# A four-layer graph network on one core: VectorE's one-hot order in the first layer's edge loop

## The reference, cut to what matters

```python
xl = (x @ W_l + b_l).reshape(n, HEADS, C);  xr = (x @ W_r + b_r).reshape(n, HEADS, C)
e = (edge_attr @ W_e).reshape(-1, HEADS, C)
g = jax.nn.leaky_relu(xl[src] + xr[dst] + e, 0.2)
logits = jnp.einsum('ehc,hc->eh', g, att)
ex = jnp.exp(logits - segment_max(logits, dst)[dst])
alpha = ex / (segment_sum(ex, dst)[dst] + 1e-16)
out = segment_sum(xl[src] * alpha[..., None], dst) + bias
```

## Time and profile before

| | |
|---|---|
| runs of the kernel | 6460.43, 6465.83, 6470.49 us (median 6465.83) |
| the profiled execution | 6478.12 us, its span 6476.2 us |
| the edge loop, first gather to last | 438.3 to 2844.3 us, 28 turns of 85.9 us |
| busy over the whole span | PE 78%, weight loads 67%, DVE 46%, ACT 28%, POOL 60% |
| TensorE's mean granted clock | 0.731 of full, over the whole span |

### The profile page before, as it was taken

The page is one execution under the profiler, slowest core; times in us unless marked ns, Lnnn a source line. Parts: engine busy times, 40 slices in busy tenths (PEclk is TensorE's granted clock), DMA queues, the critical chain, the costliest instruction groups (busy, mean ns, idle before and its releaser), DMA issues. The chain is left out here.

```text
span 6476.2 us, 113947 instructions
## 1 busy us (share of the span) xinstructions
PE 5047.6 (78%) x35178; PEld 4313.9 (67%) x35178; DVE 2978.9 (46%) x3937; ACT 1845.2 (28%) x3914; POOL 3856.6 (60%) x3427
## 2 busy tenths in 40 slices
PE   2328888888888888870799967888787788885899
PEld 2315665666555665550799967778777777774899
DVE  7657877777777777755422131111111111112321
ACT  0015555555555455530000002222222222221100
POOL 5747887888888888853000017777777777776000
PEclk9667888888888888865899975555555555555799
DMA  9325555555555555531799946666667666664598
GB/s 358 83 79 141 154 144 148 155 153 144 149 150 152 142 152 153 155 97 36 259 366 366 364 143 215 202 206 201 201 204 208 207 205 204 205 209 122 228 397 329
DMA packets 622991, 1260.53 MB, mean 195 GB/s; under 512 B 131705, under 2 KB 431290, under 8 KB 597220
## 3 DMA queue, kind: packets, MB, share of 16 engines
q10 hardware_dynamic: 217740, 649.85, 31.5%
q1 hardware_dynamic: 295768, 492.49, 21.2%
q0 software_dynamic: 109184, 115.05, 8.6%
HBM read 923.85 MB, written 490.51 MB: 218 GB/s over the span
## 5 line engine op out<-in xcount | busy, mean ns | idle before, releaser
L697 POOL DMA_INDIRECT att_gl<-tab_l,top_zero x1568 | 1928.4, 1230 | 488.5 <-issue 475.6
L1177 POOL DMA_INDIRECT sum_gl<-tab_l,top_zero x1568 | 1547.4, 987 | 517.5 <-issue 477.6
L930 ACT ACTIVATE att_acc<-att_pc 128x392 bf16<-128x392 f32 x2352 | 1088.0, 497 | 1326.7 <-PE att_pc L713 1201.3
L710 PE MATMUL att_pc<-att_ohl,att_ohv 128*128 128x392 bf16 x2352 | 867.5, 369 | 260.9 <-DVE att_ohl L810 260.8
L1105 PE MATMUL sum_pm<-sum_msg,sum_S 128*128 128x64 f32 x3136 | 683.6, 413 | 388.8 <-ACT sum_msg L1145 388.8
L713 PE MATMUL att_pc<-att_acc,att_ohv 128*128 128x392 bf16 x2352 | 861.4, 366 | 116.2 <-ACT att_acc L930 112.7
L1105 PEld LDWEIGHTS sum_pm<-sum_msg,sum_S 128*128 128x128 f32 x3136 | 657.8, 321 | 421.6 <-ACT sum_msg L1145 219.1
L1075 DVE TENSOR_TENSOR sum_t<-sum_pb,sum_gl 128x512 f32<-128x512 f32 x196 | 135.6, 692 | 1659.3 <-DMA sum_gl<-tab_l,top_zero 1276.0
L1087 PE MATMUL sum_pb<-sum_wbs,sum_ea 64*128 64x64 f32 x3136 | 694.5, 419 | 28.1 <-DMA sum_ea<-in_ea64T 28.1
L729 PEld LDWEIGHTS att_pl<-att_xe,att_S 128*128 128x128 f32 x3136 | 603.9, 218 | 161.2 <-issue 138.7
L1087 PEld LDWEIGHTS sum_pb<-sum_wbs,sum_ea 64*128 64x128 f32 x3136 | 676.1, 329 | 39.7 <-DMA sum_ea<-in_ea64T 28.3
(11 more groups left out here) (373 smaller groups left out, 5268.7 us busy)
## 6 DMA issues: line engine op xcount, KB each, us to landing
A<-att_acc SPq DMA_DIRECT2D x2352, 98.0 KB
l_a<-A SPq DMA_DIRECT2D x147, 1568.0 KB, 9.3
att_dall<-in_dst ACTq DMA_DIRECT2D x224, 448.0 KB
sum_dall<-in_dst ACTq DMA_DIRECT2D x196, 512.0 KB, 7.1
hop_at<-AT SPq DMA_DIRECT2D x56, 1568.0 KB
sum_a<-A ACTq DMA_DIRECT2D x49, 1568.0 KB, 10.2
AT<-sum_at ACTq DMA_DIRECT2D x49, 1568.0 KB, 6.4
l_at<-AT SPq DMA_DIRECT2D x42, 1568.0 KB
```

Source lines behind the costliest of these rows:

```text
L697: nc.gpsimd.indirect_dma_start(out=gl[s][:, k * GQ + j, :], out_offset=None, in_=g.tab_l, in_offset=bass.IndirectOffsetOnAxis(ap=g.ix[:, c ...
L710: nc.tensor.matmul(pc[c][m % 2][:, 0:LO], ohv[c][h][:, m, :, 0], ohl[c][h][:, m // 2, :, m % 2], start=True, stop=False)
L930: nc.scalar.activation(acc[c][n % CR][:, :], pc[c][m % 2][:, 0:LO], ACT.Copy).then_inc(s_acc[c], 1)
L1177: nc.gpsimd.indirect_dma_start(out=gl[n % RB][:, j, :], out_offset=None, in_=g.tab_l, in_offset=bass.IndirectOffsetOnAxis(ap=g.ix[:, c:c + ...
```

## The change

`items` is split. `item_rows` is the row one-hot alone, `item_lows` is the low one-hot with the wait for the buffer. `logits` is split too: its sum into `t1` becomes `joined`. The order of VectorE's list in a slot becomes: `S`; lows of chain 0, lows of chain 1; rows of chain 0; softmax or messages where they were; the sum `t1` of group n - 1; rows of chain 1; the three logits instructions. No instruction is added or taken away, and no other engine's list changes.

```diff
-                def items(i, t, c):
+                def item_rows(i, t, c):
+                    h, w = t % 2, SLOTS[t]
+                    n0 = i * (CB * CJ) + (c * CI + at0[t])
+                    v.tensor_tensor(ohv[c][h][:, 0:w, :, :], ..., ALU.is_equal).then_inc(s_oh[c], 1)
+
+                def item_lows(i, t, c):
                     h, w = t % 2, SLOTS[t]
                     n0 = i * (CB * CJ) + (c * CI + at0[t])
                     if not known(i, 1) or t >= 2:
                         dve.wait_ge(s_mm[c], i * (CB * CJ) + (at0[t - 1] if t >= 2 else (-SLOTS[SL - 1], 0)[t]))
-                    v.tensor_tensor(ohv[c][h][:, 0:w, :, :], ..., ALU.is_equal).then_inc(s_oh[c], 1)
                     v.tensor_tensor(ohl[c][h][:, 0:w // 2, :, :], ..., ALU.is_equal).then_inc(s_oh[c], 1)
 
-                def logits(i, n, b, s, k):
-                    step = InOrder(dve, s_step, n * 3 + (b * 4 + 4))
+                def joined(i, n, s, k):
                     dve.wait_ge(s_pl, n + 1)
                     dve.wait_ge(s_gl[s][k], i * (16 * GQ) + 16 * GQ)
                     v.tensor_tensor(t1[:, :, :], pl[k % 2]..., gl[s]..., ALU.add).then_inc(s_t1, 1)
+
+                def logits(n, b, s, k):
+                    step = InOrder(dve, s_step, n * 3 + (b * 4 + 4))
                     dve.wait_ge(s_t1, n + 1)
...
                         same(i, t)
                         for c in range(CH):
-                            items(i, t, c)
+                            item_lows(i, t, c)
+                        item_rows(i, t, 0)
                         if k == 1 and known(b, 1):
                             v.memset(apart[:, :], 0.0).then_inc(s_step, 4)
                         elif k == 1:
                             softmax(b - 1, i * SL + (t - 1))
                         if k == 2 and not known(b, 1):
                             messages(b - 1, 1 - s)
+                        n = i * SL + (t - 1)
                         if t:
-                            logits(i, i * SL + (t - 1), b if k else b - 1, s if k else 1 - s, (k - 1) % NQ)
+                            joined(i, n, s if k else 1 - s, (k - 1) % NQ)
                         elif not known(i, 1):
-                            logits(i - 1, i * SL + (-1), b - 1, 1, NQ - 1)
+                            joined(i - 1, n, 1, NQ - 1)
+                        item_rows(i, t, 1)
+                        if t or not known(i, 1):
+                            logits(n, b if k else b - 1, s if k else 1 - s, (k - 1) % NQ)
```

More of the change, by code:

```diff
@@ L800, in same @@
                                     ALU.is_equal).then_inc(s_S, 1)
-                def items(i, t, c):
+                def item_rows(i, t, c):
+                    h, w = t % 2, SLOTS[t]
+                    n0 = i * (CB * CJ) + (c * CI + at0[t])
+                    v.tensor_tensor(ohv[c][h][:, 0:w, :, :], spread(c_row2[:, :, :].unsqueeze(1), [P, w, P, 2]),
+                                    spread(g.vals[:, bass.ds(n0, w), :].unsqueeze(2), [P, w, P, 2]), ALU.is_equal)\
+                        .then_inc(s_oh[c], 1)
+                def item_lows(i, t, c):
                     h, w = t % 2, SLOTS[t]
@@ L806, in items @@
                         dve.wait_ge(s_mm[c], i * (CB * CJ) + (at0[t - 1] if t >= 2 else (-SLOTS[SL - 1], 0)[t]))
-                    v.tensor_tensor(ohv[c][h][:, 0:w, :, :], spread(c_row2[:, :, :].unsqueeze(1), [P, w, P, 2]),
-                                    spread(g.vals[:, bass.ds(n0, w), :].unsqueeze(2), [P, w, P, 2]), ALU.is_equal)\
-                        .then_inc(s_oh[c], 1)
                     v.tensor_tensor(ohl[c][h][:, 0:w // 2, :, :], spread(c_lo2[:, :, :].unsqueeze(1), [P, w // 2, LO, 2]),
@@ L865, in turn @@
                             messages(b - 1, 1 - s)
+                        n = i * SL + (t - 1)
                         if t:
-                            logits(i, i * SL + (t - 1), b if k else b - 1, s if k else 1 - s, (k - 1) % NQ)
+                            joined(i, n, s if k else 1 - s, (k - 1) % NQ)
                         elif not known(i, 1):
-                            logits(i - 1, i * SL + (-1), b - 1, 1, NQ - 1)
+                            joined(i - 1, n, 1, NQ - 1)
+                        item_rows(i, t, 1)
+                        if t or not known(i, 1):
+                            logits(n, b if k else b - 1, s if k else 1 - s, (k - 1) % NQ)
                 turns(dve, TURNS, turn)
-                logits(TURNS - 1, NBT * NQ - 1, LAST, LAST % R, NQ - 1)
+                joined(TURNS - 1, NBT * NQ - 1, LAST % R, NQ - 1)
+                logits(NBT * NQ - 1, LAST, LAST % R, NQ - 1)
                 softmax(LAST, NBT * NQ)
```

## The result

The changed kernel takes 6623.56 us (median of 4 runs, 6621.08 to 6633.26) against 6467.03: a ratio of 1.0246, 95% interval 1.0228 to 1.0264. It is slower, as forecast, but by 157 us where 322 were forecast, less than half. The profiled execution's span is 6621.8 us against 6476.2.

The account below looks back on a forecast made before the run. POOL's gathers were taken to bound the kernel at 85.9 us a turn; PE's stretches 64.3, gaps 19.8 and clock losses 13.4 made 97.4, so 11.5 more over 28 turns added 322 to 6465.8: 6788 us, eight in ten 6560 to 6960.

Parts of the forecast that it names:

- POOL bounds the kernel before, and the clock's falls are hidden there: Edge loop before: POOL's gathers set 85.9 us a turn; PE's clock at 0.86 of full costs nothing.
- PE stands for chain 1's rows behind `t1`: Every slot, last expand to chain 1's first item: PE waits for these row one-hots; gaps sum to 19.8 us a turn.
- the two large gaps: Ahead of chain 1's first item in slots 2 and 6, where messages precede `t1`: 4.45 and 4.18 us.
- A turn of 84.0 at full clock: Edge loop: PE's stretches of 64.3 us plus gaps of 19.8, before any loss to the clock.
- The clock's term: PE's clock falls after standing: 3.1 us lost for slot 2, 5.5 for slot 6, 4.8 for 2 us gaps; 13.4 a turn.
- The price of 0.46 per low us: PE at half clock: slot 7 takes 14.79 us against 8.01 for slot 3, so 0.46 us lost per us.
- The four 2 us gaps: PE's gaps in slots 0, 1, 4, 5: one and a half more clock falls of 7 us, 4.8 us a turn.
- 28 turns: Edge loop: growth of 11.5 us a turn, taken 28 times, adds 322 us.
- the far slower rival: Most gaps bring clock falls, lasting through slots 7 and 3: a turn of 110.6, 7157 us; chance 0.10.
- The rival that the clock holds: PE's clock stays full through its gaps: a turn of 84.0, 6412 us, faster; chance 0.08.
- POOL gains by the lows' order, hidden: Low one-hots back to back hold gathers less, some 7 us a turn by the port rule; hidden as POOL stops bounding.
- the gate: Every slot: PE waits for chain 1's row one-hots, which wait for `t1`; gaps of 19.8 us a turn.

Follow-up runs that it names:

- e6: The kernel before with six gathers per group instead of seven, the seventh chunk's rows of `gl` set to zero: 6354.09 us, ratio 0.9830.
- e5: The kernel before with 17 added matmuls, results unread, on PE ahead of slot 7's first item: 6458.26 us, ratio 0.9979.
- e2: The kernel before with only chain 1's row one-hots moved behind the sum `t1`, chain 0 in its old order: 6577.97 us, ratio 1.0161.
- e4: The changed kernel with added matmuls, results unread, on PE between both chains' first items, 18 in slots 2 and 6, 5 elsewhere: 6395.61 us, ratio 0.9872.
- e3: The changed kernel, but in slots 2 and 6 chain 1's row one-hots come right behind chain 0's, ahead of messages and `t1`: 6645.75 us, ratio 1.0262.
- e1: The kernel before with low one-hots of both chains back to back, then both chains' row one-hots, ahead of `t1`: 6303.88 us, ratio 0.9725.

## Why the prediction was right in its sign and wrong in its size

- **POOL bounds the kernel before, and the clock's falls are hidden there.** Right: e6 and e5.
- **PE stands for chain 1's rows behind `t1`.** Right: the two large gaps to 0.01, the others within 0.3, the sum 19.0 for 19.8. By slot, 0 to 7, forecast 2.10, 2.0, 4.45, 1.42, 2.10, 2.0, 4.18, 1.52; measured 2.11, 1.70, 4.44, 1.32, 2.00, 1.91, 4.18, 1.32. In slots 3 and 7 `t1` starts 0.04 after the last expand, where the prediction had 0.15. e2 shows that the second half of the change does it alone.
- **A turn of 84.0 at full clock.** Right: e4, 83.7.
- **The clock's term, 13.4 us a turn: this is the step that failed.** That the clock falls was right, the size was not: 29 low us forecast, 24.4 measured, and the granted clock of a turn did not go to 0.8 but stayed at 0.87. Measured by slot (stretch after less the full-clock stretch of the prediction): slot 2 lost 1.6, slot 6 2.2, slot 0 3.0, slot 3 1.6, slot 4 0.6; 8.9 in all, or 8.5 by e4. So the term was 4.5 us a turn too large; the gaps' sum was 0.8 too large. Three things were off.
  - For slot 6 I took 12 us between two rows (6.8 and 23.9) and 5.5 lost; it was 6.8 every time, the row that lay in a slot 6.
  - The price of 0.46 per low us was read from a slot 7, and charged to every low us. It held in slots 0 and 3 (3.0 for 6.4, 1.6 for 3.4). In slot 2, 6.3 low us cost 1.6, in slot 6, 6.8 cost 2.2. But of these 1.5 and 1.2 us lay in the gap, where PE stands anyway; in the stretches it was 4.8 and 5.6, so 0.34 and 0.39 per us. Against e4, where these stretches run at full clock, PE's idle time inside them fell from 1.81 to 1.57 in slot 2 and from 0.38 to 0.12 in slot 6: slower matmuls took up part of PE's waits, and that covers some half of what is left; the rest isn't shown.
  - The four 2 us gaps were priced at 4.8, and the slots other than 2 and 6 lost 5.2, but that is luck: slots 1 and 5 lost nothing, and 1.6 came in slot 3, whose gap is 1.32 and was priced at none. Which gap brings a fall isn't shown.
- **28 turns.** 92.2 - 85.9 = 6.3 us a turn by 28 would be 176, but 85.9 is over all turns and 92.2 over turns 2 to 27. Compared alike, those 26 grew by 6.0 on average. The first, which lacks the messages and sums of earlier batches, grew by 1.7, and the last was 3.5 shorter. From PE's first item to its last expand the loop grew by 153.5 (2408.0 to 2561.6); the medians differ by 157.
- **A misreading beside the sum.** Against the far slower rival the prediction says that PE stood 1.1 us ahead of 1507.61 and 1.7 ahead of 1517.18; by the earlier trace rows these gaps are 0.96 and 1.56. No term of the sum uses them.
- **The rival that the clock holds** would have been right about the time, 6412, had it happened: e4 makes it happen and takes 6396. The far slower rival didn't come, though e3 shows its mechanism: a fall at the head of slot 7 stays through it in 18 of 26 turns. In the changed kernel that happens in slot 3, in 4 of 26.
- **POOL gains by the lows' order, hidden.** Right, and more than hidden: its worth, 168 us or 6.0 a turn where the rival had some 7, shows once the gate is taken away (e1). The change is a gain of 2.7% and, on top of that, a loss of 5.4% (1.0246 against 0.9725) in one.

## What to carry to other kernels

When an engine that works strictly in order waits for the last of several preparations, a reordering that puts one of them behind something made by that same engine closes a ring: its length is paid in every round, however short the moved instruction. Price a stand of TensorE twice, for itself and for the clock after it; the second price depends on which work follows, so take it from rows in that very place, leave out the low time that falls into the stand itself, and check what else already sets the pace before calling either a loss. Of a change with two halves, run each alone: here one was worth keeping.

## What the runs showed of the hardware

The holding of a gather follows VectorE's instructions more exactly than I had expected. In the kernel before, gathers that begin while a low one-hot runs (446 of 1568) carry 282 us of the 454 that all gathers together take above 0.94 each, and those that begin in `S` (some 200) another 103. Those in `t1`, which has one input in PSUM (115), and those in the reduction with its one input (108), carry 0.4 us in all, each of the two groups. A held gather ends 0.82 after the instruction that holds it.

Two scans of the softmax make a pair for comparison: line 839 has two inputs in SBUF, line 837 has one of its two in PSUM. Each takes 0.42 alone. First line 839 with a gather that begins 0.16 later, then the same with a gather that begins 0.01 later, then line 837 with one that begins 0.03 later:

```profile
1316.45 0.42 DVE L839 TENSOR_TENSOR_SCAN att_top<-att_apart,att_fw 112x128 f32<-112x128 f32 x1
...
1526.58 0.46 DVE L839 TENSOR_TENSOR_SCAN att_top<-att_apart,att_fw 112x128 f32<-112x128 f32 x1
```

```profile
1316.61 1.01 POOL L697 DMA_INDIRECT att_gl<-tab_l,top_zero  x1 [0.30 <-issue]
...
1526.59 0.94 POOL L697 DMA_INDIRECT att_gl<-tab_l,top_zero  x1 [0.31 <-issue]
```

```profile
1487.20 0.42 DVE L837 TENSOR_TENSOR_SCAN att_fw<-att_apart,att_pt 112x128 f32<-112x128 f32 x1 [1.87 <-PE att_pt L737]
```

```profile
1487.23 0.94 POOL L697 DMA_INDIRECT att_gl<-tab_l,top_zero  x1 [0.31 <-issue]
```

In all 17 cases of the first kind the gather takes 1.00 to 1.02 and ends 0.75 after the scan. In the 24 in which the two begin within 0.02 of each other the gather takes its 0.94 and the scan is the one that is longer, 0.44 to 0.47. In the 8 with line 837 neither is longer. The scan holds too, then; it costs little (1.3 us in all) because it is short.

The Trainium skill (SBUF — State Buffer, "SBUF: two separate sides") counts any VectorE operation with two SBUF inputs as a holder against a GpSimd operation that reads SBUF. The comparisons and products with two SBUF inputs agree, 1.86 for 0.94, and so does this scan, 1.01 for 0.94.

TensorE's clock came back after 6.8 us in slot 6 whenever the fall lay at its head (changed kernel), and stayed down for the whole 14.8 us of slot 7 in 18 of 26 turns when it lay there (e3), with PE busy 14.73 of 14.80 us in the window shown. Both slots have four items per chain; slot 6 has only the expands beside them, slot 7 the message sums too. Which part of this work brings the clock back isn't shown.
